# Inverse of the chunk matrices by blocks of 16, with a new order of the steps of the attention part

## The reference

```python
kb   = k * beta
attn = where(strict_lower, -(kb @ k.T), 0)         # 32 x 32
T    = inv(eye - attn)                             # unit lower triangular
u, w = T @ (v * beta), T @ kb
# scan over the 8 chunks of a sequence, state S of 32 x 32:
u_i  = u0 - w_i @ S
o_i  = q_i @ S + tril(q_i @ k_i.T) @ u_i
S    = S + k_i.T @ u_i
```

## Time and profile before

| | |
|---|---|
| median of 3 runs | 440.77 us (439.73 to 440.98) |
| profiled execution, own time | 442.02 us |
| its span in the trace | 440.3 us |
| mean granted TensorE clock | 0.907 |
| TensorE busy | 371.1 us (84%), 4132 matmuls |
| VectorE busy | 294.8 us (67%), 461 instructions |
| ScalarE busy | 277.7 us (63%), 434 |
| GpSimd busy | 41.9 us (10%), 103 |
| chain that ended last | TensorE 58%, VectorE 26%, issue 7%, ScalarE 7% |

### The profile page before, as it was taken

One profiled execution on the slowest core, in us unless ns is written; L12 is line 12 of the kernel. 1 busy time (PEld: TensorE's weight loads), 2 busy tenths in 40 slices (PEclk: granted clock), 3 DMA queues, 4 the chain that ended last, 5 costly groups with the idle time before them and its releaser, 6 DMA issues.

```text
span 440.3 us, 9783 instructions
## 1 busy us (share of the span) xinstructions
PE 371.1 (84%) x4132; PEld 278.6 (63%) x4132; DVE 294.8 (67%) x461; ACT 277.7 (63%) x434; POOL 41.9 (10%) x103
## 2 busy tenths in 40 slices
PE   5599999999999998899488489366599687978996
PEld 3377776678866876799377376233267465556885
DVE  2796679628216845699696968667868696578433
ACT  4788956879677776383243265451576838558973
POOL 4000000000000100000788400000000000000000
PEclk9899999999999996889956889585999898989999
DMA  8900007400000000071600001600000000001001
GB/s 272 333 1 2 2 0 227 111 1 1 1 1 0 0 2 3 4 214 49 173 5 4 1 4 36 230 1 1 0 1 3 1 0 2 0 1 49 3 1 48
DMA packets 14325, 19.75 MB, mean 45 GB/s; under 512 B 960, under 2 KB 9152, under 8 KB 14272
## 3 DMA queue, kind: packets, MB, share of 16 engines
q1 hardware_dynamic: 14128, 18.94, 14.4%
q10 hardware_dynamic: 144, 0.01, 0.0%
HBM read 17.91 MB, written 1.05 MB: 43 GB/s over the span
## 4 chain that ended last, share of the span: by engine, by line
PE 58%; DVE 26%; issue 7%; ACT 7%; DMA 1%; DVEq 0%; SPq 0%; ACTq 0%
PE ps_a L723 11%; PE ps_a L724 11%; PE ps_a L827 8%; PE ps_a L894 2%; PE ps_a L884 2%; DVE arena L1074 2%; DVE arena L1071 2%; PE ps_d L794 2%; PE ps_d L858 2%; PE ps_a L917 2%; DVE acts L1121 2%; PE ps_d L724 2%; PE ps_d L723 2%; PE ps_d L894 2%; DVE hbuf L1116 2%
## 5 line engine op out<-in xcount | busy, mean ns | idle before, releaser
L723 PE MATMUL ps_a<-acts,w_f 128*128 128x512 f32 x256 | 103.6, 405 | 9.1 <-ACT acts L597 8.5
L724 PE MATMUL ps_a<-acts,w_f 128*128 128x512 f32 x256 | 101.7, 397 | 0.0
L723 PEld LDWEIGHTS ps_a<-acts,w_f 128*128 128x128 f32 x256 | 49.2, 192 | 22.6 <-ACT acts L597 10.2
L724 PEld LDWEIGHTS ps_a<-acts,w_f 128*128 128x128 f32 x256 | 49.2, 192 | 10.9 <-issue 0.7
L597 ACT ACTIVATE acts<-ps_a,vec 128x512 fp32r<-128x512 f32 x64 | 44.6, 697 | 0.0
L827 PE MATMUL ps_a<-xnp,conv_w 128*128 128x512 f32 x156 | 38.5, 404 | 0.0
L1140 DVE TENSOR_TENSOR acts<-gbuf,acts 128x512 fp32r<-128x512 f32 x32 | 21.6, 689 | 24.9 <-ACT acts L597 24.9
L1140 DVE TENSOR_TENSOR acts<-ghbuf,acts 128x512 fp32r<-128x512 f32 x32 | 21.2, 689 | 20.8 <-ACT acts L597 20.8
L827 PEld LDWEIGHTS ps_a<-xnp,conv_w 128*128 128x128 f32 x156 | 29.3, 188 | 8.2 <-issue 1.4
L987 DVE SCALAR_TENSOR_TENSOR arena<-ps_d,arena 128x512 f32<-128x512 f32 x16 | 11.0, 686 | 30.4 <-ACT arena L551 26.3
L594 ACT ACTIVATE gbuf<-ps_a,vec 128x512 f32<-128x512 f32 x32 | 22.3, 697 | 10.3 <-PE ps_a L724 10.2
(11 more groups left out here) (211 smaller groups left out, 778.5 us busy)
## 6 DMA issues: line engine op xcount, KB each, us to landing
toep<-in_fir SPq DMA_DIRECT2D x24, 288.0 KB, 6.5
w_in<-in_h SPq DMA_DIRECT2D x4, 1024.0 KB, 8.2
g_rows<-in_gW SPq DMA_DIRECT2D x4, 640.0 KB, 6.7
w_in<-in_w SPq DMA_DIRECT2D x6, 256.0 KB, 4.7
iobuf<-in_x SPq DMA_DIRECT2D x4, 256.0 KB, 6.5
toep<-in_taps SPq DMA_DIRECT2D x1, 768.0 KB, 6.7
y<-iobuf SPq DMA_DIRECT2D x3, 256.0 KB, 2.4
toep<-in_proj SPq DMA_DIRECT2D x1, 256.0 KB, 8.6
```

The lines of the kernel that those rows point to most:

```text
L723: e.matmul(bank, w, hi, start=start, stop=False)
L724: return e.matmul(bank, w, lo, start=False, stop=stop)
```

## The change

The inverse is computed inside the two diagonal blocks of 16 alone, by 15 steps of substitution that do both blocks in one instruction. T is then block diagonal. The corner is put in by TensorE with the right-hand side: `zz` multiplies T with (values, keys) and keeps the upper 16 rows (a scale of 1 or 0 for each partition, `top`); `ww` multiplies that with L (whose columns 0 to 15 of the transposed copy GpSimd clears, `cut`), and VectorE subtracts it from (values, keys) in place; `yy` multiplies T with the result. VectorE does both halves. GpSimd's loop goes.

The order of `att_steps` is new from the fourth FIR step on. Buffers are laid anew (states, `aqs`, statistics), the weights of the second feed-forward part are asked for after the last FIR step.

```diff
-SPLIT = 4
+SOLVED = (4, 6, 9, 12, HB - 1)
...
-    s += fir[0:4] + [("gram", 2, 1), ("lmat", 2, 1), ("solve", 2, 2), ("xt", 2, 0)]
-    s += [("token", 2, i) for i in (0, 1, 4, 5, 8, 9, 2, 3, 6, 7, 10, 11)]
-    s += [("window", 2, i) for i in range(8, 16)] + fir[4:12]
-    s += [("yy", 2, k) for k in range(4)] + [("turn4", 2, 0), ("turn4", 2, 1), ("sq", 2, 0), ("sq", 2, 1)] + sums(0)
-    s += [("aq", 2, 0), ("r1", 2, 1), ("aq", 2, 1), ("r2", 2, 1), ("aq", 2, 2), ("r3", 2, 1), ("aq", 2, 3), ("sq", 2, 2),
-          ("bo", 2, 0), ("bo", 2, 1), ("sq", 2, 3), ("bo", 2, 2), ("bo", 2, 3)] + sums(2) + [("r1", 2, 3), ("first", 2, 0)]
-    beside = {1: [fir[12], ("r2", 2, 3)], 2: [fir[13], ("r3", 2, 3), ("sq", 2, 4)], 3: [fir[14], ("r1", 2, 4)],
-              4: [fir[15], ("numbers", 2, 0)], 5: [("r2", 2, 4)], 6: [("r3", 2, 4)], 7: []}
+    s += fir[0:4] + [("solve", 2, 1), ("gram", 2, 1), ("lmat", 2, 1)]
+    s += [("token", 2, i) for i in (0, 1, 4, 5, 8, 9)] + [("zz", 2, k) for k in range(4)]
+    s += [("turn4", 2, 0)] + [("ww", 2, k) for k in range(4)] + [("solve", 2, 2)]
+    s += [("yy", 2, k) for k in range(4)] + [("token", 2, 10), ("token", 2, 11)]
+    s += [("aq", 2, k) for k in range(4)] + [("solve", 2, 3)] + [("bo", 2, k) for k in range(4)] + [("xt", 2, 1), ("first", 2, 0)]
+    beside = {1: [("token", 2, 2), ("token", 2, 3), ("turn4", 2, 1)], 2: [("token", 2, 6), ("token", 2, 7), ("r1", 2, 0)],
+              3: [("window", 2, i) for i in range(8, 12)] + [("r2", 2, 0), ("numbers", 2, 0)], 4: [("window", 2, i) for i in range(12, 16)] + [("sq", 2, 0)],
+              5: [fir[4], ("r3", 2, 0)], 6: [fir[5], ("sq", 2, 1), ("r1", 2, 1)], 7: [fir[6], ("r2", 2, 1)]}
     for n in range(1, NCH):
         s += [("rec", 2, n)] + beside[n]
-    s += [("turn3", 2, 0), ("sq", 2, 5), ("xt", 2, 1)] + [("yy", 2, k) for k in range(4, 8)] + sums(5) + [("turn", 2, 0)]
-    s += [("sq", 2, 6), ("sq", 2, 7), ("aq", 2, 4), ("aq", 2, 5), ("gate", 2, 0), ("gate", 2, 1)] + sums(6) + sums(7)
-    s += [("aq", 2, 6), ("aq", 2, 7), ("sq", 2, 8), ("logit", 2, 0), ("logit", 2, 1), ("r1", 2, 8), ("r2", 2, 8)]
-    s += [("bo", 2, b) for b in range(4, 8)]
+    s += [("turn3", 2, 0), fir[7], ("sq", 2, 2), ("r3", 2, 1)] + [("zz", 2, k) for k in range(4, 8)] + sums(2)
+    s += [("sq", 2, 3), ("ww", 2, 4), ("ww", 2, 5), ("ww", 2, 6), ("ww", 2, 7)] + [("yy", 2, k) for k in range(4, 8)] + sums(3)
+    s += [("sq", 2, 4)] + fir[8:10] + sums(4) + [("sq", 2, 5)] + [("bo", 2, k) for k in range(4, 8)] + sums(5) + fir[10:16]
+    s += [("turn", 2, 0)] + [("aq", 2, k) for k in range(4, 8)]
...
-    s += [("lturn", 2, 0), ("soft", 2, 0), ("round", 2, 0), ("r3", 2, 8), ("prob", 2, 0), ("mul", 2, 0), ("first", 2, 1),
-          half[1], ("addmix", 2, 0), ("mul", 2, 1), half[2], ("add", 2, 1), ("osq", 2, 1), half[3], ("rms", 2, 0),
-          half[4], ("scale", 2, 0), half[5], ("wo", 2, 0), half[6], ("wo", 2, 1), half[7], ("turn3", 2, 1), ("sq", 2, 9)]
-    s += sums(9)
+    s += [("first", 2, 1), ("gate", 2, 0), ("sq", 2, 6), half[1], ("gate", 2, 1), ("r1", 2, 6), half[2], ("sq", 2, 7), ("r2", 2, 6),
+          ("logit", 2, 0), ("r3", 2, 6), half[3], ("logit", 2, 1)] + sums(7) + [("sq", 2, 8), ("lturn", 2, 0), ("soft", 2, 0)]
+    s += [half[4], ("round", 2, 0), ("r1", 2, 8), ("prob", 2, 0), ("mul", 2, 0), half[5], ("mul", 2, 1), ("addmix", 2, 0),
+          ("add", 2, 1), ("osq", 2, 1), half[6], ("r2", 2, 8), ("rms", 2, 0), half[7], ("r3", 2, 8), ("scale", 2, 0),
+          ("turn3", 2, 1), ("wo", 2, 0), ("wo", 2, 1), ("sq", 2, 9)] + sums(9)
...
-STATS = ((4, 0), (0, 0), (1, 0), (2, 0), (4, 1), (3, 0), (0, 1), (1, 1), (2, 1), (3, 1))
+STATS = ((4, 0), (4, 1), (0, 0), (1, 0), (2, 0), (3, 0), (0, 1), (1, 1), (2, 1), (3, 1))
...
-            e.wait_ge(S["pe_a"], A_AT[("logit", 2, 1)] + 1)
+            e.wait_ge(S["pe_a"], A_AT[("fir", 2, FIR_ORDER[15])] + 1)
             load_weights(e, w_in[1], S["ld_w2"], S["ld_h2"], S["ld_h2"])
...
+            e.memset(alt[0][:, :, :, 0, 0:HB], 0.0).then_inc(S["cut"], 1)
...
+                if p < 3:
+                    e.wait_ge(S["act_a"], A_AT[("fir", 2, FIR_ORDER[8 * g + 7])] + 1)
+                    e.activation(yu[:, i // 4, i % 4].rearrange("p n c -> p (n c)"), bank[:, :], ACT.Identity,
+                                 scale=vc("top")).then_inc(S["act_a"], 1)
...
+                elif kind == "ww":
+                    g, h = i // 4, i % 4
+                    e.wait_ge(S["cut"], g + 1)
+                    e.wait_ge(S["act_a"], A_AT[("zz", 2, i)] + 1)
+                    bank = take_d(dd)
+                    for n in range(NCH):
+                        for b in range(4):
+                            r = slice(32 * b, 32 * b + 32)
+                            last = e.matmul(bank[r, 64 * n:64 * n + 64], alt[g][r, h, n, 0], yu[r, g, h, n],
+                                            start=True, stop=True)
+                elif kind in ("zz", "yy"):
+                    if kind == "zz":
+                        e.wait_ge(S["inv_done"], g + 1)
+                        e.wait_ge(S["act_a"], A_AT[("token", 2, (9, 7)[g])] + 1)
+                    else:
+                        e.wait_ge(S["dve_d"], D_AT[("ww", 2, i)] + 1)
...
+                    k = HB - 1 - j
+                    shape = [128, 2, k, j + 1]
+                    own(e.tensor_tensor(prod, lblk[g][:, :, j + 1:HB, j:j + 1].to_broadcast(shape),
+                                        tblk[g][:, :, j:j + 1, 0:j + 1].to_broadcast(shape), ALU.mult))
                     own(e.tensor_tensor(sub, sub, prod, ALU.subtract))
...
+                        if i and h == H - 1:
+                            turn_inverse(0)
+                        if i and h < H - 1:
+                            substitute(SOLVED[h + 1], SOLVED[h + 2])
+                elif kind == "ww":
+                    v = vk[:, i // 4, i % 4].rearrange("p n x c -> p (n x c)")
+                    e.wait_ge(S["pe_d"], dd + 1)
+                    e.tensor_tensor(v, v, ps_d[:, dd % NRING], ALU.subtract).then_inc(S["dve_d"], 1)
```

More of the change, by code:

```diff
@@ L103 @@
 RING_A = {"in": 1, "flag": 1, "gsum": 1, "up": KT, "hid1": KT, "hid2": KT, "out": 1, "qkv": 4, "window": 1, "token": 1, "fir": 1,
-          "yy": 1, "bo": 1, "gate": 2, "logit": 1, "addmix": 1}
-RING_D = {"mean": 1, "var": 1, "up": KT, "down": 1, "sumsq": 2, "gram": H, "aq": 1, "rec": 1,
+          "zz": 1, "yy": 1, "bo": 1, "gate": 2, "logit": 1, "addmix": 1}
+RING_D = {"mean": 1, "var": 1, "up": KT, "down": 1, "sumsq": 2, "gram": H, "ww": 1, "aq": 1, "rec": 1,
           "wo": 1}
@@ L433, in _ @@
             own(e.tensor_copy(pick[:, 16:20], head_w[:, 0:128:32]))
+            own(e.memset(vc("top"), 0.0))
+            for q in range(4):
+                own(e.memset(vec[32 * q:32 * q + HB, V["top"]:V["top"] + 1], 1.0))
             e.tensor_scalar(pick[:, 16:19], pick[:, 16:19], 1.0 / DH, None, ALU.mult).then_inc(S["mask_done"], 1)
@@ L875, in _ @@
                     last.then_inc(S["pe_a"], 1)
-                elif kind == "yy":
+                elif kind == "ww":
                     g, h = i // 4, i % 4
-                    e.wait_ge(S["inv_done"], g + 1)
-                    e.wait_ge(S["act_a"], A_AT[("token", 2, 11)] + 1)
+                    e.wait_ge(S["cut"], g + 1)
[6 more added lines that the diff above has]
+                                            start=True, stop=True)
+                    last.then_inc(S["pe_d"], 1)
+                elif kind in ("zz", "yy"):
[5 more added lines that the diff above has]
+                        e.wait_ge(S["dve_d"], D_AT[("ww", 2, i)] + 1)
                     bank = take_a(a)
@@ L905, in _ @@
                             r = slice(32 * h, 32 * h + 32)
-                            last = e.matmul(bank[r, 64 * b:64 * b + 64].rearrange("p (x t) -> p x t", x=2), s_sb[r, g, b],
-                                            aqs[g][r, b, n], start=True, stop=True)
+                            last = e.matmul(bank[r, 64 * b:64 * b + 64].rearrange("p (x t) -> p x t", x=2), s_sb[g][r, b],
+                                            aqs[r, b, n], start=True, stop=True)
                     last.then_inc(S["pe_d"], 1)
@@ L1177, in _ @@
                             "p (n a t) -> p n a t", n=NCH, a=2)[:, :, 1], mk, ALU.mult).then_inc(S["dve_d"], 1)
-                        if i:
-                            substitute(SPLIT + h, SPLIT + h + 1)
+                        if i and h < H - 1:
+                            substitute(SOLVED[h + 1], SOLVED[h + 2])
                 elif kind == "lmat":
-                    turned = e.transpose(lmat[i].rearrange("p i j -> p (i j)"),
-                                         alt[i][:, :, :, 0, :].rearrange("p h n t -> p t (h n)"))
-                    if i:
-                        turned.then_inc(S["l_turned"], 1)
-                    else:
-                        own(turned)
+                    e.transpose(lmat[i].rearrange("p i j -> p (i j)"),
```

(13 more changed lines are left out.)

85 lines of the change are left out of this document (40 added, 45 removed).

## The result

The changed kernel takes 480.21 us (median of 4 runs, 478.27 to 480.74), the kernel before 440.88 beside it. The ratio is 1.0888, with a 95% interval of 1.0849 to 1.0926: 39 us slower. The profiled execution has a span of 477.6 us against 440.3, so 37.3 us of difference can be looked at in the two traces.

A forecast was written before the change was run, and what follows sets the result against it. The prediction took TensorE's chain of small products in attention as the bound, at 26 ns a pass: +32.4 us before the gates less 5 behind, +27.4 on the profiled 442.02 gives 469.4, as median 468; range 450 to 484.

The forecast's parts named there:

- What bounds the kernel: Attention part: both substitutions cost nothing by themselves; from 210 on TensorE's chain of small products is long, with fetch gaps.
- (a): Half 0's inverse out at about 190.5 instead of 210.05; zz starts at 192.1, 18.0 us earlier than yy did.
- (b): Half 0's zz, ww, yy, aq, bo: 1248 passes, 32.4 us plus 1.3 for two tokens; first state transposition ends at 226.7.
- The two rows of 22.3 ns: Paces read before the change: 256 passes of the second gram, and 256 after an idle time without a gap.
- Halfway between: Second support for 26 ns a pass: it lies halfway between the paces measured with gaps, 22.3 and 30.1 ns.
- (c): Seven scan (rec) steps with the work beside them: 19.9 us, so zz 4 starts at 246.6.
- (d): Half 1's zz, ww, yy: 768 passes, 20.0 us, to 266.6; then FIR steps and bo to 281.9.
- (e): Last toep load, behind FIR 15, takes 5.5 us: a new TensorE stall of 2.6 us; aq ends at 293.2.
- (f): First gate product at 293.3, before 260.94: pre-gate sum +32.4 us; VectorE idle from about 277 to about 288.
- (g): First gate to end of last statistics turn: 50 us counted, 55.9 before; 5 us taken back, between 0 and 14.
- the rival that costs more than the passes: 31 ns a pass (+12.5 us), and the half clock falls on gates and mixing products: 480 to 486; chance 0.16.
- the rival of a late corner: ww waits for GpSimd's cleared copy or VectorE's half-1 substitution; serial order costs rather than passes: 472; chance 0.05.
- the rival of cheap passes: Instruction fetch keeps ahead, all 2496 passes before the gates run at 15.8 ns: 432 to 440; chance 0.08.

The follow-up runs named there:

- experiment 4: Kernel before with GpSimd's substitution loop left out, so half 1 is not inverted: 442.13 us, ratio 0.9984.
- experiment 5: Kernel before with the last 16 of VectorE's 31 substitution steps left out, so half 0 is only partly inverted: 441.54 us, ratio 0.9978.
- experiment 8: Kernel before without the last two toep reloads (groups 0 and 1 for half 1) and the FIR steps' waits for them: 441.62 us, ratio 0.9989.
- experiment 12: Kernel before with two VectorE steps reordered: half 1's inverse turned before path 3's turn, its first state before the first mixing product: 440.70 us, ratio 0.9980.
- experiment 2: Kernel before with each yy product issued three times, repeat outside the loop over the four blocks, so neighbouring passes use different array parts: 472.29 us, ratio 1.0698.
- experiment 1: Kernel before with each yy product issued three times in a row into the same place, 1024 more passes: 486.17 us, ratio 1.0981.
- experiment 6: Changed kernel with the eight last FIR steps put between half 1's zz, ww and yy, same work: 476.87 us, ratio 1.0768.
- experiment 7: Changed kernel with FIR steps between half 1's small products, and the second feed-forward weights' load released only after the last aq: 471.90 us, ratio 1.0670.

## Why the prediction was right or wrong, point by point

- **What bounds the kernel: right.** Both substitutions are off the path (experiments 4, 5). One limit belongs to it: GpSimd's end was 2.8 us ahead, and in experiments 8 and 12 it was late at once.
- **(a) The start of zz: right.** 192.03 for 192.1, with VectorE's steps at 0.24 to 0.33 an instruction and the turn of half 0 over at 190.3 for 190.5.
- **(b) Half 0's chain: this is the step that failed, by 5 us.** First state at 231.85 for 226.7. 1248 passes took 37.4 us (192.03 to 231.18, less 1.7 for two tokens), 30.0 ns each for the 26 taken. Two things lie on this stretch, though the text had a row for each. The toep reload of 187 to 196 lies on zz and made a gap of 3.97. After it TensorE runs at a granted clock of 0.60 on the mean (210 to 232), so that 127 passes take 3.0 to 3.2 us instead of 2.0, with gaps of 0.4 to 2.0 beside. The clock is what was mis-sized: all gaps from 192 to 231 together, the 3.97 among them, are 10.8 us, less than the 13.0 that the forecast's 10.4 ns a pass gives for 1248, while the passes themselves took 26.6 us, 21.3 ns each for 15.8. The row nearest to that, 30.1 ns a pass from 219.87 to 234.33, was at a granted clock of 0.50 throughout and beside no load; I took the full clock's pace for a stage that had lost it. The two rows of 22.3 ns had nothing in common either: the second gram's 210 passes ran at full clock and stopped for 1.49 us, yy's 256 ran without a gap at a granted clock of 0.64. "Halfway between" them was no second reason for 26 ns.
- **(c) The scan: right.** From the first state to zz 4, 19.0 us for 19.9.
- **(d) zz, ww, yy of half 1: right.** 768 passes in 20.1 us, 26.2 ns each for 26, at a granted clock of 1.00: pieces of 1.99 us, gaps of 1.45 to 1.73. In parts it is 15.6 ns bare and 10.5 ns of gaps, the forecast's 15.8 and 10.4.
- **(e) The load: right in kind, short in size.** TensorE waited 3.93 us for toep, not 2.6, bo took 8.7 us for 6.7 with a gap of 3.59 beside the first reload, aq 6.5 for 5.8. The forecast said that a gap can be longer there and gave it nothing: some 4.5 us in all from the end of yy 7 to the first gate.
- **(f) First gate at 302.02 for 293.3**, the sum of (b) and (e). VectorE's idle time before the statistics turn is 19.5 us; nobody waited for it, since the turn ended at 298.6 and TensorE was in aq until 302.
- **(g) Behind the gates: 52.5 us for 50.** VectorE is busy 40.4 of them. The mixing products took 7.61 us at a mean granted clock of 0.59 (before, 6.68 at 0.68), and VectorE's part of the fourth scan step of half 1 stood behind the softmax's work, for which TensorE waited 5.37 us.

The sum in the trace is 41.1 - 3.4 = 37.7 us for 27.4 forecast. The measured 480 us are 12 above the forecast's 468. They lie in the range stated, at the rival that costs more than the passes (480 to 486), not in the forecast's own 462 to 475: the direction and the terms were right, the number was not. That rival named 31 ns a pass and the half clock; what it had is seen in half 0 (30.0 ns at a mean granted clock of 0.70), for half 1 it isn't so (26 ns). No experiment changed the clock alone, so its price here is read from rows. That passes are cheap is excluded (experiment 2: 29.7 ns), and so is the rival of a late corner: VectorE waited for TensorE at each ww, 17 us in all. Two sums of the prediction are slightly off, and nothing hangs on them: the scan's terms in (c) add up to 19.75 us, and in the rival of cheap passes (b) ends at 213.1, not 212.7.

That the gaps are the fetch of instructions is inferred; no view shows the fetch of one block. It rests on four findings: they come after 127 or 128 passes in a long run (of the three that the prediction lists, the 1.11 us are none of them, as said above); the instruction queue has 8 packets and 0.13 MB more than before (52 for 44, 0.85 MB for 0.72) for 2048 instructions of TensorE more (a product and a weight load a pass), so 256 instructions, or 128 passes, to a packet; they vanish where the pace is slower (experiments 1, 6); they grow beside a data load and shrink without it (7, 8). The Trainium skill ("Runtime: NRT & Kernel Launch", Instruction fetch mechanics) says that an engine's instructions are refilled by DMA in blocks of 16 KiB, 256 instructions. The runs agree with the block's size. What isn't settled is how far ahead TensorE fetches: after a pause or other work 176 to 252 passes ran without a gap at full clock, and 307 at a mean of 0.73 (experiment 2, half 1). Nor is it why some gaps beside a load stay short.

## What to carry to other kernels

A substitution that is hidden behind another engine is worth nothing to shorten; look at who is busy beside it before its work is handed to the engine that hides it. Price small matmuls by a long run of them in the trace, gaps included (here 26 ns a pass at full clock and 30 at the lower one, where the bare row at full clock says 16), look at the granted clock of the row that a price is taken from, and mark every data load that runs beside one. When work is moved, follow the loads that it releases too: in experiment 6 two loads came to lie on runs of small products and took back part of what the move had won.

## What was not expected of the hardware

- Three products in a row on one 32x32 part of the array, into one place in PSUM, cost 37.0 ns a pass, against 23.0 (2.92 us for 127) when neighbours use different parts, both at a granted clock of 0.50. At full clock the latter take 15.6 (1.98 us for 127); for the former there is no row at full clock. And the clock was 0.50 over 27 us in which TensorE was busy without a break.
- VectorE's products and subtractions of two operands in SBUF wait for GpSimd's: 0.63 us instead of 0.20 for 31 elements, and yy 0 came 11.8 us later (221.92 for 210.11). The Trainium skill ("SBUF — State Buffer", Who interferes with whom) says that the port pair which the two engines share is an exclusive lock, and that a VectorE instruction with two inputs in SBUF contends with a GpSimd one that reads SBUF; the run agrees. In the kernel before, GpSimd starts when VectorE's substitution is over, and its reductions beside it take 1.21 us, as without.
- "Issue" gaps of 3 to 5 us that begin while the DMA engines are full (share 1.04 at 194 to 195 us) with a data load, and end after it, some 2.4 us in the first case.
